# Eight batches of a macaron block on one Trainium2 core: second attentions take turns with first ones from the fourth batch on, and the linear attention's y products move one phase later

## The reference, cut to what matters

```
x = x + 0.5 * ffn(layernorm(x))     # "first attention": softmax, 16 heads of width 16
x = x + attn(layernorm(x))          # linear attention, 8 heads, no softmax
x = x + 0.5 * ffn(layernorm(x))     # "second attention": the same weights as the first

ffn(x):  q, k, v = x @ Wq, x @ Wk, x @ Wv
         z = softmax(q k^T / 16) v          # per head, 1024 x 1024 scores
         z = l2norm(z @ Wo); z = l2norm(z @ Wff); return gelu(z)
attn(x): out = (q k^T) v per head, then out @ w_o^T + b_o      # all of it linear
```

## Time and profile before

| | |
|---|---|
| median of three runs | 2878.8 us |
| profiled execution | 2880.11 us, its span 2878.3 us |
| start, up to the first exponential | 51.7 us |
| a LINEAR phase (3) | 184.1 us |
| a PLAIN phase (11) | 167.8 us |
| TensorE, VectorE, ScalarE, GpSimd busy | 93%, 93%, 94%, 30% |
| mean granted TensorE clock | 0.984 |

### The profile page before, as it was taken

How to read it: one execution, slowest core, us unless ns; L and a number is a source line. 1 busy time by engine, 2 the same in 40 slices (tenths; PEclk the granted TensorE clock), 3 DMA queues, 4 the chain that set the end, 5 groups by cost and what they waited for, 6 DMA issues and landing times.

```text
span 2878.3 us, 87462 instructions
## 1 busy us (share of the span) xinstructions
PE 2668.9 (93%) x35680; PEld 1073.0 (37%) x35680; DVE 2668.2 (93%) x5390; ACT 2713.5 (94%) x5031; POOL 865.7 (30%) x1389
## 2 busy tenths in 40 slices
PE   5899999999999999999999999999989899998987
PEld 2233443434434344344443443333323333333422
DVE  4999898998989989899899999999999999999997
ACT  3999999999999999999999999999999999999997
POOL 2324204333143331432424313132331313233111
PEclk8999999999999999999999999999999999999999
DMA  5231242323422334123341243422324342232440
GB/s 125 51 81 29 52 104 50 72 44 60 105 38 53 75 60 102 31 53 84 60 96 32 52 92 60 93 59 56 81 44 101 60 98 54 56 80 45 86 89 16
DMA packets 151363, 192.90 MB, mean 67 GB/s; under 512 B 34001, under 2 KB 85713, under 8 KB 150962
## 3 DMA queue, kind: packets, MB, share of 16 engines
q1 hardware_dynamic: 150386, 186.13, 31.6%
q0 software_dynamic: 576, 1.18, 0.3%
HBM read 36.18 MB, written 16.78 MB: 18 GB/s over the span
## 4 chain that ended last, share of the span: by engine, by line
PE 35%; ACT 31%; DVE 26%; issue 6%; POOL 1%; SPq 1%; DMA 0%; DVEq 0%; ACTq 0%; POOLq 0%
ACT exp_ring L593 25%; DVE exp_ring L678 21%; PE ring L784 12%; PE ring L838 10%; PE o_acc L849 10%; PE ring L889 2%; ACT w_xn L604 2%; ACT xn_T L612 1%; DVE bn_stats L718 1%; ACT kq_stage L627 1%; DVE w_xn L695 1%; ACT ring L599 1%; DVE v_now L751 1%; ACT L604 1%; SPq L430 1%
## 5 line engine op out<-in xcount | busy, mean ns | idle before, releaser
L678 DVE TENSOR_SCALAR_CACHE_REDUCE exp_ring<-ring 128x1024 f32<-128x1024 f32 x2048 | 2410.0, 1214 | 117.9 <-PE ring L838 109.5
L593 ACT ACTIVATE exp_ring<-exp_ring,neg_max 128x1024 f32<-128x1024 f32 x2048 | 2333.0, 1143 | 89.8 <-DVE exp_ring L678 87.2
L838 PE MATMUL ring<-kq_stack 128*32 128x512 bf16 x16384 | 1175.2, 383 | 124.3 <-DVE exp_ring L678 81.7
L849 PE MATMUL o_acc<-exp_ring,v_scaled 128*32 128x512 f32 x8192 | 1080.1, 600 | 34.7 <-POOL v_scaled L546 25.1
L838 PEld LDWEIGHTS ring<-kq_stack 128*32 128x32 bf16 x16384 | 406.7, 96 | 1038.4 <-DVE exp_ring L678 417.9
L546 POOL TENSOR_TENSOR v_scaled<-v_now,exp_rsums 128x64 f32<-128x64 f32 x512 | 150.1, 293 | 1764.3 <-DVE exp_rsums L688 1746.5
L593 ACT ACTIVATION_READ_ACCUMULATOR exp_ring<-exp_ring,neg_max 128x1 f32 x2048 | 387.9, 189 | 0.0
L849 PEld LDWEIGHTS o_acc<-exp_ring,v_scaled 128*32 128x32 f32 x8192 | 252.7, 111 | 253.9 <-POOL v_scaled L546 43.8
L784 PE MATMUL ring<-ffn_wo_wowff,o_T 128*32 128x256 f32 x4096 | 244.1, 380 | 15.4 <-DVE o_T L685 14.1
L784 PE MATMUL ring<-xn_T,ffn_wqkv 128*32 128x512 f32 x2048 | 249.0, 607 | 8.0 <-DVE exp_ring L678 6.7
L784 PEld LDWEIGHTS ring<-ffn_wo_wowff,o_T 128*32 128x32 f32 x4096 | 133.1, 110 | 125.1 <-DVE exp_ring L678 26.1
(11 more groups left out here) (99 smaller groups left out, 1249.2 us busy)
## 6 DMA issues: line engine op xcount, KB each, us to landing
kq_stack<-kq_parts SPq DMA_DIRECT2D x2030, 64.0 KB, 2.4
x_post<-in_L_attn_x SPq DMA_DIRECT2D x8, 1024.0 KB, 8.6
x_slots<-x_post SPq DMA_DIRECT2D x8, 1024.0 KB, 5.4
x_prep<-x_slots SPq DMA_DIRECT2D x8, 1024.0 KB, 8.7
x_post<-x_slots SPq DMA_DIRECT2D x8, 1024.0 KB, 5.8
x_prep<-in_L_attn_x SPq DMA_DIRECT2D x7, 1024.0 KB, 9.1
out<-x_post SPq DMA_DIRECT2D x7, 1024.0 KB, 5.7
kq_stack<-kq_parts POOLq DMA_DIRECT2D x18, 64.0 KB, 4.6
```

The lines of the kernel that those rows point to most:

```text
L593: nc.scalar.activation(e, e, ACT.Exp, bias=negmax[:, i % NM:i % NM + 1], scale=-1.0, accum_out=sums[:, g % EG, c:c + 1]).then_inc(exp_done, 1)
L678: nc.vector.tensor_scalar(E[:, (g % EG) * HQ + c, :].rearrange("p (b n) -> p b n", b=NB), ps, -1.0, None, ALU.mult, ALU.min, accum_out=neg ...
L838: last = mm(ps[k:k + COLS, n, :], kq[:, 0, c, j * P + k:j * P + k + COLS], kq[:, 1, c, n * BANK:(n + 1) * BANK], start=True, stop=True)
L849: last = mm(O[32 * c:32 * c + 32, n, :], vsc[a][:, g % EG, c, :], E[:, (g % EG) * HQ + c, n * BANK:(n + 1) * BANK], start=(a == 0 and j == ...
```

## The change

It does three things. The order of the phases: first attentions of batches 0, 1, 2; then second and first in turns (second of 0, first of 3, second of 1, ...); then the second attentions of batches 5, 6 and 7. So first attentions are phases 0, 1, 2, 4, 6, 8, 10, 12. The tables: a phase whose predecessor was a first attention is LINEAR if it is phase 1, 2 or 13, else SPREAD (3, 5, 7, 9, 11); the others are SHARED (4, 6, 8, 10, 12) or PLAIN (0, 14, 15). In SPREAD y stands at places 132.8 to 153.6, that is at t5, t12, t19 and t25 of the SHARED phase behind it, with the last xbias and the store; T, VK, G and H stand later than in LINEAR, gram nearly where it was. The read-outs z and v that lie in a LINEAR phase stay on ScalarE; those in SPREAD phases are on VectorE, as in PLAIN. Waits that counted phases of the linear kind by p now count by `nth_linear(p)` or `linear_before(p)`.

```diff
+    FIRST, SECOND, AHEAD_BY = 0, 1, 3
+    TURNS = [(FIRST, b) for b in range(AHEAD_BY)] + [
+        turn for b in range(B - AHEAD_BY) for turn in ((SECOND, b), (FIRST, b + AHEAD_BY))] + [
+        (SECOND, b) for b in range(B - AHEAD_BY, B)]
+    LINEAR_PHASES = [p for p, turn in enumerate(TURNS) if turn[0] == FIRST]
+    def is_linear(q):
+        return q in LINEAR_PHASES
+    def batch(p):
+        return TURNS[p][1]
+    def nth_linear(p):
+        return LINEAR_PHASES.index(p)
+    def linear_before(p):
+        return LINEAR_PHASES[nth_linear(p) - 1]
...
         "PLAIN": {
...
-            "u": (8.7, 10.9, 12.4, 21.6, 29.9, 42.2, 55.8, 58.2),
+            "u": (8.7, 10.9, 12.4, 21.6, 29.9, 42.3, 52.4, 57.2),
...
         "LINEAR": {
...
-            "T": (63.6,),
-            "VK": (70.8,),
-            "G": (76.3,),
-            "H": (87.1,),
-            "xbias": (90, 90.2, 110.8, 112.2),
-            "y": (104.6, 109.3, 116.3, 120.3),
+            "T": (63.7,),
+            "VK": (70.9,),
+            "G": (72.4,),
+            "H": (87.4,),
+            "xbias": (90.3, 90.9, 110.5, 116.4),
+            "y": (104.7, 110.2, 116.3, 118.6),
...
+        "SPREAD": {
+            "recip": 5.5,
+            "av": 8.1,
+            "av_next": 2,
+            "z": 5.4,
+            "u": (11.3, 13.4, 16.8, 17.7, 17.9, 21.8, 25.3, 27.2),
...
+            "gelu": (32.3,),
+            "x1": (36.1, 36.6, 36.9, 36.9),
...
+            "xn2": (41, 43.6, 43.8, 44.7, 46.5, 47.2, 49.3, 49.9),
+            "gram": (54.4, 58.1),
+            "xt2": (66.3, 101.1),
+            "T": (69.7,),
+            "VK": (71,),
+            "G": (86.5,),
+            "H": (105.6,),
+            "xbias": (119.7, 121.1, 122.5, 133.5),
+            "y": (132.8, 140, 147.5, 153.6),
...
+            "qk": (79.2, 82.4, 94.2, 98.5, 32.1, 35.2, 38.4, 41.3),
+            "v": (111.3, 122.4, 125.6, 5.7),
+            "load_xp": (2,),
+            "stack1": (52,),
+            "load_xr": (42.8,),
+            "stack2": (72.4,),
+            "stack3": (98.4,),
+            "stack0": (104,),
+            "store": (143.5,),
+        },
+        "SHARED": {
...
+            "av": 9.1,
...
+            "z": 4.9,
+            "u": (9.4, 10.8, 13.1, 23.6, 30.9, 42.1, 55.9, 61.8),
...
+            "gelu": (67.5,),
...
+            "xt": (65.6, 68.3),
+            "qk": (76.6, 89.5, 92.5, 96.7, 16.9, 21.6, 34.3, 39.5),
+            "v": (115.2, 120.6, 126.9, 7.5),
+            "load_xp": (7.7,),
+            "stack1": (10.8,),
+            "load_xr": (27.3,),
+            "stack2": (29.4,),
+            "stack3": (36.6,),
+            "stack0": (112.8,),
+            "store": (132.5,),
+        },
         "TAIL": {
-            "u": (7.9, 8.9, 14.5, 30.4, 31.7, 51.3, 53.3, 67.3),
-            "u_norm": (17.5, 71.5),
+            "u": (10.1, 14.7, 18.4, 22.5, 33.3, 49.9, 51.6, 59.2),
+            "u_norm": (24.5, 65.7),
...
-    GAP = {'gram': 0.5, 'y': 0.5, 'VK': 0.5, 'G': 0.5}
+    GAP = {'gram': 0.5, 'y': 0.5, 'VK': 0.5, 'G': 1.0}
...
-            "dve": {"ln_stats": -1.0, "z": -2.0, "w_norm": 0.5, "ln2_stats": 0.5, "H": -0.5, "VK": -0.5, "T": 0.5},
+            "dve": {"ln_stats": -1.0, "z": -2.0, "w_norm": 1.0, "ln2_stats": 0.5, "VK": -0.5, "T": 0.5},
...
+    def kind_of(p):
+        if is_linear(p - 1):
+            return "LINEAR" if p < AHEAD_BY or p == PHASES - AHEAD_BY else "SPREAD"
+        return "SHARED" if AHEAD_BY < p < PHASES - AHEAD_BY else "PLAIN"
...
-    ON_ACT = {step for place, step in steps if step[0] in ("z", "v") and 1 <= place // TILES <= B}
+    ON_ACT = {step for place, step in steps if step[0] in ("z", "v") and 0 <= place < PHASES * TILES
+              and kind_of(int(place // TILES)) == "LINEAR"}
...
-                    if p >= B:
-                        sp.wait_ge(stored, 16 * (p - B + 1))
-                    sp.dma_start(xp[:], tokens(x_in[p] if p < B else xs[p - B])).then_inc(xp_loaded, 16)
+                    if not is_linear(p):
+                        sp.wait_ge(stored, 16 * (LINEAR_PHASES[batch(p)] + 1))
+                    sp.dma_start(xp[:], tokens((x_in if is_linear(p) else xs)[batch(p)])).then_inc(xp_loaded, 16)
```

More of the change, by code:

```diff
@@ L68, in build_macaron @@
             "z": 4.7,
-            "u": (8.7, 10.9, 12.4, 21.6, 29.9, 42.2, 55.8, 58.2),
-            "u_norm": (63.4,),
-            "w_norm": (66,),
-            "gelu": (67,),
-            "x1": (69.8, 70.4, 72, 72.3),
-            "ln_stats": (5.8, 7.9, 9, 9, 10.5, 10.5, 16.1, 16.2),
-            "ln_aggr": (25.6,),
-            "ln_rstd": (32.3,),
-            "xn": (35.1, 35.9, 42.1, 45.5, 46.3, 46.8, 47, 47),
-            "xt": (62.2, 66.6),
-            "qk": (76.9, 84.2, 90.1, 101.7, 17.9, 25.6, 33.3, 37.3),
-            "v": (117.8, 123.9, 127.4, 3.4),
-            "load_xp": (3.6,),
-            "stack1": (5.9,),
-            "load_xr": (7.8,),
-            "stack2": (40,),
-            "stack3": (81.5,),
-            "stack0": (107.7,),
-            "store": (113.4,),
+            "u": (8.7, 10.9, 12.4, 21.6, 29.9, 42.3, 52.4, 57.2),
+            "u_norm": (62.9,),
+            "w_norm": (66.9,),
+            "gelu": (67.8,),
+            "x1": (70, 70.3, 71.5, 72.7),
+            "ln_stats": (5.8, 7.7, 7.9, 9, 9.9, 10.5, 15.4, 16.2),
+            "ln_aggr": (26,),
+            "ln_rstd": (32.4,),
+            "xn": (39.4, 40, 40.8, 47, 49.6, 50.4, 51.2, 51.8),
+            "xt": (62.2, 66),
+            "qk": (77.1, 84.2, 90.1, 97.5, 18.1, 25.6, 33.2, 37.4),
+            "v": (117.2, 123.3, 126.8, 5.6),
+            "load_xp": (1.5,),
+            "stack1": (7.4,),
+            "load_xr": (9,),
+            "stack2": (26.8,),
+            "stack3": (78.7,),
+            "stack0": (102.1,),
+            "store": (131.9,),
         },
@@ new lines, in build_macaron @@
+            "u": (11.6, 12.5, 14.9, 16.1, 17.4, 21.2, 25.3, 27.2),
+            "u_norm": (27.4,),
+            "w_norm": (32.8,),
+            "gelu": (32.9,),
+            "x1": (35, 35, 36.3, 36.4),
+            "ln2_stats": (36.3, 36.9, 37.3, 37.8, 38.7, 38.7, 38.8, 39),
+            "ln2_aggr": (39.5,),
+            "ln2_rstd": (44,),
+            "xn2": (43, 43.8, 43.9, 44.1, 45.5, 46, 49.5, 50),
+            "gram": (54.4, 58),
+            "xt2": (66.8, 101.4),
+            "T": (63.7,),
@@ L147, in build_macaron @@
     PARTS = {"u": 2, "qk": 2, "v": 2, "y": 2, "gram": 4, "T": 3, "VK": 2, "G": 2, "H": 3}
+    def kind_of(p):
+        if is_linear(p - 1):
+            return "LINEAR" if p < AHEAD_BY or p == PHASES - AHEAD_BY else "SPREAD"
+        return "SHARED" if AHEAD_BY < p < PHASES - AHEAD_BY else "PLAIN"
     def table(p):
-        return TABLES["START"] if p < 0 else TABLES["TAIL"] if p == PHASES else \
-            TABLES["LINEAR"] if 1 <= p <= B else TABLES["PLAIN"]
+        return TABLES["START"] if p < 0 else TABLES["TAIL"] if p == PHASES else TABLES[kind_of(p)]
     steps = []
@@ L474, in _ @@
                     sp.wait_ge(x1_done, chunk(p, (i + 1) * CHUNKS // n - 1))
-                    sp.dma_start(tokens(out[p - B])[:, rows, :], xr[:, rows, :]).then_inc(stored, 16)
+                    sp.dma_start(tokens(out[batch(p)])[:, rows, :], xr[:, rows, :]).then_inc(stored, 16)
                 elif kind in ("stack0", "stack1", "stack2", "stack3"):
@@ L864, in _ @@
                     if kind == "xt2":
-                        pe.wait_ge(xn2_ready, (p + 1) * NT)
+                        pe.wait_ge(xn2_ready, (nth_linear(p) + 1) * NT)
                     elif p >= 1:
```

131 lines of the change are left out of this document (69 added, 62 removed).

## The result

The changed kernel takes 2914.8 us (median of four runs, 2913.3 to 2917.4) against 2880.3 (four runs, 2876.0 to 2882.1) for the kernel before: a ratio of 1.0124, 95% interval 1.0112 to 1.0135. The forecast was 2866 with a range of 2845 to 2889, so the prediction is wrong in sign and outside its range.

The account below looks back on a forecast made before the run. No single engine was taken to bound the kernel; each stretch had its own. Seven steps summed to -2.6 us a pair, five pairs to -13, from 2880.1 to 2867.1, or 2866 for a median; range 2845 to 2889.

Parts of the forecast that it names:

- (f): SHARED t0 to t32: y comes in and TensorE becomes the bound; +3.3 us, bounds +2.4 and +5.2.
- (c): SPREAD t64 to t96: T comes in, H leaves, a z moves to VectorE; -0.7 us, bounds -2 and +1.
- (d): SPREAD t0 to t32: z and v read-outs go from ScalarE to VectorE; -0.5 us, bounds -1 and +1.5.
- (a): SPREAD t96 to t128: y leaves, H comes in, VectorE becomes the bound; -2.7 us, bounds -4.0 and -1.
- (b): SPREAD t48 to t64: T moves out, taking work off TensorE; -2.0 us, bounds -2.1 and 0.
- (e): SPREAD t32 to t48: keeps its list (gelu, x1, second statistics); 0 us, bounds -2 and +1.
- (g): Rest of SHARED: plain list with a u and xt three tiles later; 0 us, bounds -1 and +1.
- a head start: SHARED t0 to t32: entering with the three-slot ring full is worth about one tile, 1.3 us off 48.8.
- (1): Rival: SHARED's crowded first quarter decides, +5.2 us there; +3.0 a pair, +15, 2894; chance 0.17.
- (2): Rival: balance works over whole phases of SPREAD and SHARED; -5.2 us a pair, -26, 2853; chance 0.15.
- (3): Rival: ScalarE bounds both kinds of phase, only work off it counts; -3.7 us a pair, -18, 2860; chance 0.13.
- (4): Rival: SHARED t0 to t32 takes what the stretches t0 to t32 and t48 to t128 of SPREAD give; 2879; chance 0.15.

Follow-up runs that it names:

- y alone: The kernel before with the new order of phases, old tables, and only y, the xbias steps and the store at SPREAD's late places: 2915.0 us, 1.0121.
- the watched y: A single y at t35 of SHARED, in the changed kernel with y moved to t5, t17, t27 and t35: 2920.0 us, 1.0144.
- the order alone: The kernel before with only the new order of phases, every table, LEAD and GAP as before: 2885.6 us, 1.002.

## Why the prediction was wrong

**The step that failed is the rule by which the quarters were priced, that a stretch takes as long as its fullest engine.** It set (f), (c) and (d), and all three ended above their upper bounds:

```
step                      forecast   bound   measured   missed by
(a) SPREAD t96 to t128      -2.7     -1.0      -1.9        0.8
(b) SPREAD t48 to t64       -2.0      0        -1.5        0.5
(c) SPREAD t64 to t96       -0.7     +1.0      +1.6        2.3
(d) SPREAD t0 to t32        -0.5     +1.5      +1.7        2.2
(e) SPREAD t32 to t48        0       +1.0       0          0
(f) SHARED t0 to t32        +3.3     +5.2      +5.7        2.4
(g) the rest of SHARED       0       +1.0      +0.5        0.5
a pair                      -2.6               +6.1        8.7
```
The five pairs average +6.3. Before, (d), (c) and (f) took 0.2, 0.6 and 0 us longer than their fullest engine was busy; now they take 1.8, 1.9 and 1.1 longer. The narrow range rested on the bounds not all being met at once; the misses all went one way.

**(f), SHARED t0 to t32.** "It enters with the ring full (the SPREAD end is VectorE's), which is worth about one tile: 48.8 - 1.3 = 47.5, +3.3", bounds +2.4 and +5.2. Measured +5.7, of which y makes 4.1, inside the bounds, and SHARED's other new places 1.6, which the forecast had at nothing; with y alone moved, +8.6. TensorE's 48.8 was right to the tenth. Two things were wrong in y's own price. The fullest engine's time was taken for the whole, though the watched y stops TensorE's score tiles first and VectorE's after them. And a head start was taken off, where the kernel before has nothing left of it by t13 (1.65 us paid for 1.7). With three slots TensorE can be two tiles ahead, 2.3 us at the pace of 1.13, and a y of 1.9 with the score matmuls behind it uses that up; this is an estimate, no run changed the slots. An upper bound of 7.0 + 2.4 = 9.4, both engines' work in full, would have held all versions. The new table, against y alone, takes the quarter from 53.0 to 49.9, so the choice of places is worth 3.1.

**(a), t96 to t128:** 40.6 for 39.8 forecast (42.5 before), -1.9 for -2.7. The mechanism was right: the chain is VectorE's from t112 on, and its wait for score matmuls in t96 to t128 is down to 0.5 us from the 2.3 of the earlier trace rows. Out of 7.0 us of matmul moved away 1.9 came back.

**(b), t48 to t64:** -1.5 for -2.0, right. **(c), t64 to t96:** +1.6 (24.0 + 20.2 against 42.6) for -0.7. The upper bound had named T and VK a tile apart; taking both back moved 2.4 us out of t64 to t80 and 1.9 into t48 to t64, which shows that these two steps carry the cost, but not whether by their wait or by their time. **(d), t0 to t32:** +1.7 (24.2 for 22.5 in t16 to t32) for -0.5, above its bound of +1.5. It was counted against phase 3, which follows a LINEAR phase. Four of the five SPREAD phases follow one of the plain kind, and there the order alone takes 47.4, as phase 1 of the kernel before did (24.9 + 22.5, also behind a plain phase), so the 47.7 is 0.3 more; phase 3, behind a LINEAR one in both, went from 46.0 to 47.8, and why stays open. **(e):** 28.2 to 30.1 over the five phases, 30.0 in the earlier trace rows: no change beyond what such phases differ by in one run (last section). **(g):** 124.1 (39.7 + 45.9 + 38.5) for 167.8 - 44.2 = 123.6, +0.5 for 0, inside its bound.

**The tables that keep their kind** were priced at nothing without reading which steps moved: measured 11 us by themselves in the old order, 5.6 in the six phases where the new kernel has them. The start's -1.8 is not START's: it takes 49.5 with the old START in the order alone and 51.3 with the new one in the tables alone. TAIL changed nothing (29.4 from the last exponential to the end in both).

**The rivals.** (1) named the place and the mechanism (first quarter over 49, c and d at their upper bounds), with 2894 and a chance of 0.17; it was 21 us short: 3.3 a pair, as every part but (e) came out a little worse than it had them, and the 5.6 of the kept tables. (2) balance over phases: TensorE's busy time in a SPREAD phase fell from 177.8 to 173.5 (170.8 foreseen) and the time didn't; out. (3) ScalarE bounds both kinds, so y's place is no matter: y alone moved costs 29 us; out. The Trainium skill, page "Perfetto Trace Analysis", section "Identifying the Most-Contended Engine", judges TensorE's headroom by the share of weight loads (with the flops), not by matmul busy time. That share is 37% of the span, and 47% around phase 9's t13 (4.45 of 9.50 us), which by that measure leaves room; the trace disagrees, as 1.7 us added to TensorE there cost 1.65. (4) zero sum: it was not; with y alone moved 2.5 came back for 8.6.

What stays open: how far the two engines' times add at a y where both have other work (8.6 of 9.4 with the old tables, 4.1 with the new); why t16 to t32 of SPREAD costs 1.7 more than in LINEAR, and phase 3 with it; how the new tables, which take 2.7 us off a SHARED phase against y alone (174.0 for 176.7), lose most of it in SPREAD (182.2 to 184.1 for 181.5); and why the order alone's other runs take up to 5 us longer than the profiled one.
